# One elementwise multiply per supertile is issued on GpSimd instead of VectorE

## The reference

```python
xn = layernorm(x)
r = sigmoid(bitlinear(xn, Wr)); k = bitlinear(xn, Wk); v = bitlinear(xn, Wv)   # ternary weights
scale = exp(positions * log(sigmoid(decay)))
state = cumsum(k * v / clip(scale, 1e-10), axis=time) * scale
s = bitlinear(rmsnorm(r * state, ln_w), Wo)
g = silu(xn + expert_w[argmax(xn @ gate_w.T)] @ xn)       # one of 8 experts for each token
out = x + s * g
```

## Time and profile before

| | us |
|---|---|
| median of the runs (two: 1245.94 and 1247.17) | 1246.56 |
| the profiled execution, its time | 1246.9 |
| the profiled execution, span of its slowest core | 1245.4 |
| spans of the eight cores | 1226.4 to 1245.4 |
| granted TensorE clock of the eight cores | 0.916 to 0.920 |
| busy: PE, VectorE, ACT, POOL | 908.5, 691.3, 453.9, 85.9 |

### The profile page before, as it was taken

One profiled execution on the slowest core, in us unless ns is written; L12 is line 12 of the kernel. 1 busy time (PEld: TensorE's weight loads), 2 busy tenths in 40 slices (PEclk: granted clock), 3 DMA queues, 4 the chain that ended last, 5 costly groups with the idle time before them and its releaser, 6 DMA issues.

```text
span 1245.4 us, 17429 instructions; the slowest of 8 cores (1226.4 to 1245.4 us)
## 1 busy us (share of the span) xinstructions
PE 908.5 (73%) x5760; PEld 552.6 (44%) x5760; DVE 691.3 (56%) x1381; ACT 453.9 (36%) x929; POOL 85.9 (7%) x220
## 2 busy tenths in 40 slices
PE   0212226666666648899999999889899899899874
PEld 0111115555555536465555554455355365365331
DVE  4777766655555346353573573473573573573543
ACT  3444443333333163503703703703712712722102
POOL 0000001111110110000000000000000000000000
PEclk9999998777777769999999999899999999999887
DMA  3333352888877883531561652561570670570760
GB/s 103 102 114 107 106 161 67 206 192 206 197 187 169 185 207 111 211 130 68 226 218 70 235 207 76 215 221 35 219 259 18 229 265 10 205 260 1 244 228 34
DMA packets 37673, 196.25 MB, mean 158 GB/s; under 512 B 5840, under 2 KB 7888, under 8 KB 30416
## 3 DMA queue, kind: packets, MB, share of 16 engines
q0 software_dynamic: 17280, 134.23, 34.7%
q1 hardware_dynamic: 20304, 60.91, 14.9%
HBM read 186.73 MB, written 25.17 MB: 170 GB/s over the span
## 4 chain that ended last, share of the span: by engine, by line
PE 57%; DVE 24%; issue 6%; DMA 6%; ACT 5%; DVEq 1%; SPq 0%; ACTq 0%; POOL 0%; POOLq 0%
PE pb L612 26%; PE pb L502 23%; DVE qwb L272 5%; PE pb L666 5%; DMA ebuf<-escr 4%; DVE sC L268 3%; PE pb L278 2%; ACT xn_fm L415 2%; DVE wvT L293 2%; DVE wkT L293 2%; DVE sC L558 2%; DMA out<-s_sb 2%; DVE sD L541 2%; DVE moe L628 1%; DVE woT L291 1%
## 5 line engine op out<-in xcount | busy, mean ns | idle before, releaser
L612 PE MATMUL pb<-ebuf,xn_fm 128*128 128x512 bf16 x2048 | 468.5, 390 | 40.9 <-DMA ebuf<-escr 20.3
L612 PEld LDWEIGHTS pb<-ebuf,xn_fm 128*128 128x128 bf16 x2048 | 203.3, 100 | 296.0 <-issue 74.4
L628 DVE SCALAR_TENSOR_TENSOR moe<-pb,ohb,moe 128x512 bf16<-128x512 f32 x224 | 167.8, 749 | 70.9 <-PE pb L612 55.9
L278 PE MATMUL pb<-identb,qwb 128*128 128x128 bf16 x384 | 48.6, 306 | 212.7 <-DVE qwb L272 212.7
L502 PE MATMUL pb<-xn_fm,wkT 128*128 128x256 bf16 x1024 | 134.9, 300 | 7.0 <-ACT xn_fm L415 7.0
L278 PEld LDWEIGHTS pb<-identb,qwb 128*128 128x128 bf16 x384 | 37.2, 137 | 223.9 <-issue 223.9
L502 PEld LDWEIGHTS pb<-xn_fm,wkT 128*128 128x128 bf16 x1024 | 109.2, 107 | 32.7 <-issue 8.9
L502 PE MATMUL pb<-xn_fm,wvT 128*128 128x256 bf16 x1024 | 114.4, 273 | 2.7 <-DVE sC L524 2.7
L502 PEld LDWEIGHTS pb<-xn_fm,wvT 128*128 128x128 bf16 x1024 | 100.1, 98 | 16.1 <-issue 3.0
L258 ACT ACTIVATE sA<-stageQ 128x1024 f32<-128x1024 f32 x48 | 50.7, 1057 | 99.4 <-DVE sC L268 96.3
L524 DVE SCALAR_TENSOR_TENSOR sC<-sB,pb 128x512 f32<-128x512 f32 x64 | 39.7, 681 | 75.8 <-PE pb L502 75.8
(11 more groups left out here) (101 smaller groups left out, 839.5 us busy)
## 6 DMA issues: line engine op xcount, KB each, us to landing
ebuf<-escr POOLq DMA_DIRECT2D x48, 2048.0 KB, 9.0
ebuf<-ewt POOLq DMA_DIRECT2D x64, 256.0 KB, 15.4
escr<-ebuf POOLq DMA_DIRECT2D x8, 2048.0 KB, 7.2
stageQ<-wk SPq DMA_DIRECT2D x16, 512.0 KB, 3.4
stageQ<-wv SPq DMA_DIRECT2D x16, 512.0 KB, 3.5
xb<-xpre SPq DMA_DIRECT2D x16, 512.0 KB, 10.9
xb<-xmain SPq DMA_DIRECT2D x16, 512.0 KB, 11.7
stageQ<-xmain SPq DMA_DIRECT2D x16, 512.0 KB, 10.0
```

The lines of the kernel that those rows point to most:

```text
L278: return [e.matmul(bank[:, i2 * 128:(i2 + 1) * 128], qwbf[:, (4 * q + i2) * 128:(4 * q + i2 + 1) * 128], ident[:], start=True, stop=True) ...
L612: ins.append(e.matmul(bank[:, 0:512], xnf[:, kc * ST + j * 128: kc * ST + (j + 1) * 128], kbuf[:, kc * D + nh * 512: kc * D + nh * 512 + 512],
L628: e.scalar_tensor_tensor(dst, bank[:, 0:512], ohcol, src2, ALU.mult, ALU.add)],
```

## The change

The multiply L575 of `emit_y` is issued on GpSimd. It reads `sD` and `sA` and writes `sB`, 128 partitions of 2048 fp32 elements, as before. It runs once in each of the eight supertiles. It keeps its place in program order, which on POOL is behind the load for e2 and ahead of the load for e3. L577, which stays on VectorE, waits for it by a semaphore of POOL, as does the ACT instruction L340 that overwrites `sA`. Nothing else changes.

```diff
@@ emit_y
                 for i in range(4)],
                 reads=[f"p{rb0 + i}" for i in range(4)], writes=["sD"])
-            op("vector", lambda e: [e.tensor_tensor(sB[:], sD[:], sA[:], ALU.mult)],
+            op("gpsimd", lambda e: [e.tensor_tensor(sB[:], sD[:], sA[:], ALU.mult)],
                reads=["sD", "sA"], writes=["sB"])
             op("vector", lambda e: [e.tensor_tensor(ybf[:], sC[:], sB[:], ALU.mult)],
                reads=["sC", "sB"], writes=["ybf"])
```

## The result

| | before | after |
|---|---|---|
| median, us | 1250.76 (10 runs) | 1263.87 (11 runs) |
| ratio, 95% interval | | 1.0105 (1.0088 to 1.0122) |
| profiled execution: time, span of slowest core | 1246.9, 1245.4 | 1265.41, 1263.9 |
| granted TensorE clock, mean over a core | 0.916 to 0.920 | 0.906 to 0.916 |

The account below looks back on a forecast made before the run. PE was taken to wait on the chain behind L575 through VectorE and ACT's layer norm. Losses of 0 (st0), 13.0 (five supertiles), 1.7 (st4) and 0.8 (st7) sum to 15.5 us: 1262, range 1252 to 1274.

Parts of the forecast that it names:

- T: The multiply's time on POOL, taken as 4.5 us, against 2.28 on VectorE; the forecast used 4.2 to 4.9.
- D: How much later all that is behind the multiply comes: T - 1.91, forecast as 2.6 us.
- Does it stay lost?: Step about what follows e3 on PE: later waits move along, so nothing later gives lost time back.
- return of 3.4 us: Low-clock stretch moving from e3 to e2 in st3 and st6, giving 3.4 us back.
- clock rival: PE idles longer ahead of e2; a second 1.2 GHz stretch costs 12 us more: 27.5, 1274; chance 0.13, dear side.
- a lower mean clock: Listed among the signs that would show the prediction wrong; no size given.
- Path (b): Layer norm chain over ACT and VectorE to e3: moves by D, covered only by ACT's idle time before L415, 5.3 us.
- path (a): VectorE's L577, L681 and evictions of e1 move by D and delay e2; in st4 1.4 hidden, e2 moves 1.2.
- term for st7: Last supertile, no layer norm: 1.8 us hidden ahead of e2, 0.8 us left.
- The cheap multiply: Rival: POOL streams as ACT does, multiply 1.9 us, nothing later, 1247; with 2.28 us, 1248; chance 0.10.
- The dear multiply: Rival: multiply takes 5.86 us on POOL, D 3.95, sum 24.9 us, 1271.5; chance 0.08.
- The late load: Rival: POOL's multiply delays the weight load for e2, about 4.3 us in each of eight supertiles: 34, 1281; chance 0.05.

Follow-up runs that it names:

- e2: Not a run: PE's work after e0 and e1 in each supertile; needs its weights loaded and PSUM banks emptied of e1.
- e0: Not a run: PE's work in each supertile whose end the load for e2 waits for.
- dve_twice: Kernel before, with the multiply L575 done twice on VectorE into the same buffer; ratio 1.0093, 1261.4 us.
- e3: Not a run: PE's work after e2 in each supertile; needs the next supertile's transposed input from the layer norm chain.
- pool_twice: Changed kernel with the multiply done twice on POOL; ratio 1.0372, 1295.9 us.
- act_free_pool: Changed kernel, with ACT's discarded output of L340 and L349 written to y2g, so L340 doesn't wait for POOL; ratio 1.0090, 1261.9 us.
- late_pool_gated: late_pool with POOL's multiply also waiting for VectorE's second add (L681), so it runs beside the evictions of e1; ratio 0.9907, 1238.1 us.
- split: Changed kernel with the multiply cut in two: POOL does the first 1024 columns, VectorE the other 1024; ratio 1.0028, 1251.9 us.
- late_pool: Against the kernel before: multiply on POOL, L577 placed behind L358, ACT's L340 and L349 writing to y2g; ratio 0.9967, 1246.5 us.
- e1: Not a run: PE's work ahead of e2 in each supertile; VectorE evicts its results from PSUM.

## Why the prediction was right, and where it was not

**Right.** 1262 against 1246.6 was forecast, +15.4 us; measured are +13.1 (11.0 to 15.3). The mechanism is as stated, but for the points below. T was 4.51 for the 4.5 taken; the start on POOL 0.54 behind the load's issue for 0.6; D 2.52 for 2.6; L577 4.82 behind e0's last eviction, forecast was about 5.0. The load for e3 was not moved. The layer norm path lost its cover: what was left of idle time ahead of L415 is 1.7 us in all, never over 0.6. By the table e3 came 2.61 us later in st1 to st6; the sum had 14.7 / 6 = 2.45. dve_twice, pool_twice and act_free_pool carry the rest of it: lateness alone, whichever engine makes it, more for more of it, and not by ACT's wait.

**"Does it stay lost?" is the step that failed in part.** Of the 2.61 us at e3, 2.03 are left at the first projection and 1.83 at the next supertile. I had written that nothing later gives any back. The first part, 0.58, lies where e3 and e4 run, 14.60 us before and 14.02 after. In the kernel before, a stretch at 1.2 GHz falls into e3 or e4 in 21 of 48 supertiles (st3: the earlier trace rows) and under e2 in the other 27. After, PE stands still for 4.4 us ahead of every e2 from st1 to st6, and the stretch is there in all 48, longer than before (e2 of st1: clock 0.68 over 8.70 us, below; 0.80 over 8.60 in st0 before), while VectorE and ACT work on the layer norm; e3 and e4 have one in 5. With it they took 15.65 us, without it 13.79, so 16 cases fewer of 48 are worth 0.6 us on average, about the 0.58:

```profile
595.20:603.90 8.70, 8.70 (x28) 0.68 0.45 190
```

```profile
605.31 2.60 ACT L415 CAST xn_fm<-pb 128x512 bf16<-128x512 f32 x4 [0.59 <-PE pb L409]
```

This is the return of 3.4 us that the prediction named for st3 and st6 inside its clock rival, and spread over more supertiles. The dear side of that rival, a second stretch in each, shows in 5 supertiles of 48, two of them on this core (st4 and st5); as a whole it didn't come. That the clock is what gives the 0.58 back is read from the timelines and not tested by a run of its own. Where the other 0.20 comes from stays open.

**A sign of being wrong that came.** The prediction named a lower mean clock as such a sign. The clock did fall, from 0.916 to 0.920 over the cores to 0.906 to 0.916, and e2 with the wait for the transposes grew from 8.18 to 9.14 us. It cost little, because the layer norm on ACT and VectorE was late by D in any case: the transposes start 2.94 us later where D is 2.52, e3 2.61. The sign was badly chosen, as a lower clock under e2 is mostly hidden and one under e3 is not. Another sign, supertile starts 2 to 3 us further apart, missed narrowly with 1.83.

**Path (b) is the longer in every supertile: not quite.** With e2 taking 9.8 us, as in st1, ACT waits 0.59 us for the transposes ahead of L415. So path (a) with the slow e2 decides there. In st1 to st6 over all cores ACT had such a wait in 27 cases of 48, of at most 0.6 us; before it had one in 10, of up to 2.3.

**Mis-sized terms.** Means over the eight cores, e3's shift: st0 0.80 where 0 was forecast, st4 2.47 where 1.7 was; core 5's idle times in these two (4.26 and 0.88) were that core's and that execution's. st7 and what follows it, from its load to the end of the span, is 94.56 after and 90.04 before, 4.5 more where 0.8 was forecast, in one execution each; dve_twice has 96.34 there. There is no next supertile's work between the visits, and on the slowest cores PE waits ahead of e2, e4 and e6: for 3.65, 2.05 and 6.59 us before, for 4.42, 3.90 and 6.75 after. The prediction counted the wait ahead of e2 alone. The clock from st7's load to the end is 0.862 before and 0.836 after (means over the cores). I didn't take this apart further. For st0 to st6 the table has 7 x 1.83 = 12.8, against 14.7 forecast. With the 4.5 at the end these two executions differ by 17.3, of which 2 to 3 belong to before's quick one. So the term for st7 was too small, the part given back was not in the sum, and that 15.4 comes so near the measured time is in part luck: the two errors have opposite signs. The range has a slip too: by the prediction's own terms T = 4.9 gives D = 2.99 and 18.2 us, not 17.6.

**The rivals.** The cheap multiply fell with T = 4.51. The dear multiply (5.86) likewise. The late load fell with landing times of 8.2, 8.1 and 8.5 us for the loads of e2, in no relation to POOL's work.

**The price of the multiply by the page.** The Trainium skill, page "GPSIMD Engine Reference", section "Elementwise — side-by-side cycle accounting", has 4497 ns for an add of this size on GpSimd; the rows show 4514 for the multiply. The trace agrees.

## What to carry to other kernels

A multiply moved off the busier engine frees nothing if the very next instruction of that engine reads its result. Look first at who waits for the product and what stands behind the waiter. Here the 2.3 us reader alone, placed behind the evictions and L358, so that it starts 5.8 us later, was worth 1.1%, with no engine changed. When such work goes to GpSimd nonetheless, give it cover of its whole length there, and let it run beside VectorE instructions with at most one SBUF input, as late_pool_gated does. Even so it gained nothing here over leaving the multiply on VectorE.

## What the hardware showed beside this

- A VectorE tensor_tensor with two SBUF inputs and a GpSimd tensor_tensor exclude each other: 1.21 us became 3.75 (split), 1.22 became 5.53 (late_pool, once 5.92), and POOL's 4.51 became 5.28. The Trainium skill, page "SBUF — State Buffer", section "Who interferes with whom", says that a VectorE instruction with two SBUF inputs contends with a GpSimd one that reads SBUF, and that the order of issue decides who is blocked. The exclusion agrees. The order doesn't: VectorE started 0.25 to 0.31 us first in the profile in every case of both kernels. In split it was blocked nevertheless in 56 cases of 64. In late_pool its first add was blocked in 8 cases of 56, all in st1, and kept its 1.21 us in the rest. What decides stays open.
- Beside evictions from PSUM with one SBUF input both engines kept their times (4.50 with 0.75; 4.50 with 0.75).
- GpSimd took its multiply 0.54 us after it had begun to issue a 2 MB DMA, and the DMA was not later for it than beside VectorE's second multiply (landing 9.4 and 10.0 us).
